# Two transfers per block instead of four for the rows of negated maxima, with the planner's costs of SP's jobs and its seeds replaced

## The reference, cut to what matters

```python
x = x + L0_attn(layernorm(x))   # one head, width 64, causal softmax
x = x + L0_ffn(layernorm(x))    # 256 x 256, inputs rounded to 8-bit floats
x = x + L1_attn(layernorm(x))   # 16 heads of width 16, rotary positions, causal softmax
x = x + L1_ffn(layernorm(x))    # sigmoid(xr Wr) * (relu(xk Wk)^2 Wv), x mixed with the row before it

scores = Q @ K^T / sqrt(d)      # per head, 2048 x 2048
scores = where(causal, scores, -inf)
out = softmax(scores) @ V
```

## Time and profile before

| | |
|---|---|
| time, median of 3 runs | 2366.51 us (2357.9 to 2366.91) |
| the profiled execution's own time | 2356.72 us |
| its span, first to last instruction | 2354.9 us |
| mean granted clock of TensorE | 0.994 of full speed |
| TensorE busy | 94% of the span |
| VectorE busy | 85% |
| ScalarE busy | 64% |
| GpSimd busy | 23% |
| DMA, mean | 53 GB/s |

### The profile page before, as it was taken

The page is one execution under the profiler, slowest core; times in us unless marked ns, Lnnn a source line. Parts: engine busy times, 40 slices in busy tenths (PEclk is TensorE's granted clock), DMA queues, the critical chain, the costliest instruction groups (busy, mean ns, idle before and its releaser), DMA issues.

```text
span 2354.9 us, 50513 instructions
## 1 busy us (share of the span) xinstructions
PE 2217.2 (94%) x19221; PEld 1031.1 (44%) x19221; DVE 2009.2 (85%) x4326; ACT 1511.1 (64%) x2753; POOL 531.2 (23%) x528
## 2 busy tenths in 40 slices
PE   7899899999999999999999999999999999999998
PEld 4555433433544444443454445444354444433354
DVE  6689899999889898888988889988887989998932
ACT  2244477676666667667656676667666677778763
POOL 5544301302322121220324212130222300000012
PEclk9999999999999999999999999999999999999999
DMA  2422411110212112021121213121021122111110
GB/s 51 115 76 60 120 49 30 42 55 13 78 45 76 42 56 73 19 78 42 31 84 42 70 37 90 33 57 57 19 55 57 38 64 68 31 36 31 30 48 30
DMA packets 185883, 125.29 MB, mean 53 GB/s; under 512 B 84912, under 2 KB 185392, under 8 KB 185648
## 3 DMA queue, kind: packets, MB, share of 16 engines
q1 hardware_dynamic: 184880, 121.16, 18.4%
q10 hardware_dynamic: 768, 0.92, 0.1%
HBM read 62.20 MB, written 59.24 MB: 52 GB/s over the span
## 4 chain that ended last, share of the span: by engine, by line
PE 61%; DVE 26%; ACT 5%; issue 3%; POOL 2%; SPq 1%; DMA 1%; POOLq 0%; DVEq 0%; ACTq 0%
DVE mx L1609 16%; PE psum L1929 15%; PE psum L1907 8%; PE psum L1875 7%; ACT probs L1372 3%; PE psum L1842 3%; PE psum L1715 2%; PE psum L1968 2%; PE psum L1777 2%; PE psum L1980 2%; PE psum L1960 2%; PE psum L1806 2%; PE psum L1746 2%; PE psum L1949 2%; PE psum L1863 2%
## 5 line engine op out<-in xcount | busy, mean ns | idle before, releaser
L1609 DVE TENSOR_REDUCE mx<-psum 128x1 f32<-128x512 f32 (+2 forms) x2304 | 1290.2, 621 | 130.4 <-PE psum L1875 89.2
L1372 ACT ACTIVATE probs<-psum 128x512 f32<-128x512 f32 x2176 | 1134.4, 607 | 325.8 <-PE psum L1907 233.3
L1929 PE MATMUL psum<-probs,vs 128*17 128x512 f32 (+3 forms) x5120 | 574.3, 535 | 1.6 <-ACT probs L1372 0.8
L1875 PE MATMUL psum<-kst,qst 48*128 48x512 f16 (+3 forms) x2560 | 425.2, 350 | 46.6 <-ACT probs L1372 16.7
L1907 PE MATMUL psum<-qst,kst 50*128 50x512 f16 (+3 forms) x2560 | 423.4, 349 | 40.9 <-DVE mx L1609 19.1
L1875 PEld LDWEIGHTS psum<-kst,qst 48*128 48x128 f16 x2560 | 127.3, 93 | 352.3 <-ACT probs L1372 127.6
L1907 PEld LDWEIGHTS psum<-qst,kst 50*128 50x128 f16 x2560 | 128.4, 93 | 331.0 <-ACT probs L1372 138.5
L1929 PEld LDWEIGHTS psum<-probs,vs 128*17 128x17 f32 x5120 | 96.3, 96 | 162.6 <-issue 123.2
L1882 PE MATMUL psum<-maskq,identh 64*128 64x64 bf16 (+1 forms) x2048 | 126.0, 202 | 0.0
L1156 POOL TENSOR_SCALAR vare<-mv 128x4 f32<-128x4 f32 x64 | 14.6, 229 | 450.9 <-DVE mv L1474 450.9
L1914 PE MATMUL psum<-maskk,identh 64*128 64x128 bf16 (+1 forms) x2048 | 112.9, 202 | 0.0
(11 more groups left out here) (173 smaller groups left out, 2820.1 us busy)
## 6 DMA issues: line engine op xcount, KB each, us to landing
qk_dram<-parts SPq DMA_DIRECT2D x168, 128.0 KB
qst<-qk_dram SPq DMA_DIRECT2D x128, 96.0 KB, 2.3
kst<-qk_dram SPq DMA_DIRECT2D x128, 96.0 KB, 2.3
v_dram<-vst SPq DMA_DIRECT2D x64, 136.0 KB, 4.0
vs<-v_dram SPq DMA_DIRECT2D x64, 136.0 KB, 2.1
xs<-x_in SPq DMA_DIRECT2D x16, 512.0 KB, 4.0
x_dram<-xs SPq DMA_DIRECT2D x16, 512.0 KB, 3.0
att_dram<-ast SPq DMA_DIRECT2D x64, 128.0 KB, 2.0
```

The lines of the kernel that those rows point to most:

```text
L1372: act.activation(dst, src, ACT.Exp, scale=DK1 ** -0.5 / LIFT ** 2).then_inc(S["exp"], 1)
L1609: ins = dve.tensor_reduce(mx1[:, n % 2, 2 * g + odd, tile % TPC, c:c + 1], bank(src, at, at + cols), AX.X, ALU.max)
L1875: ins = pe.matmul(two[odd][:, at:at + cols], qst[rows, qslot, pair, P * (tile % TPC):P * (tile % TPC + 1)], kst[rows, kslot, pair, 0:cols] ...
L1929: ins = pe.matmul(bank(7, off, CH, rows=VW, row=32 * h), vtile[:, h, :], probs[:, HG * (step_no(b, hg, k) % PSTEPS) + h, at:at + CH - off] ...
```

## The change

The rows of a block's negated maxima are laid out with the parity of head outermost and the number row next, so that 16 neighbouring partitions of `nmaxT1` go to two neighbouring partitions of `qst`. Each parity is one transfer, two per block where there were four. The waiting count per use of a slot becomes 32.

The planner gets other costs for all jobs of SP (the time for which SP is held) and for two latencies, and another list of seeds, as long as the one before. So the order of all jobs on all five engines, the bank assignments and the places of the filler matmuls are derived anew.

```diff
-SEEDS = (306, 378, 194, 6, 194, 308, 415, 291, 473, 121, 8, 110, 281, 463, 416, 413, 185, 504, 77, 23, 86, 190,
...
+SEEDS = (68, 333, 414, 370, 236, 48, 123, 291, 381, 267, 127, 221, 307, 222, 395, 39, 314, 77, 39, 284, 296,
...
-    add("SP", "load x", c, key() - (60.0 if b else 1e4), 0.1, ...
+    add("SP", "load x", c, key() - (60.0 if b else 1e4), 0.45, ...
-    add("SP", "rows0", c, key(), 0.2, ("turnmax0 d", c), ("rows0", p), last, lat=2.9)
+    add("SP", "rows0", c, key(), 1.35, ("turnmax0 d", c), ("rows0", p), last, lat=2.9)
-    add("SP", "store x2", c, key(), 0.1, ("addf", (*c, 0)), ("addf", (*c, 1)), lat=3.0)
+    add("SP", "store x2", c, key(), 0.45, ("addf", (*c, 0)), ("addf", (*c, 1)), lat=3.0)
-        add("SP", "put", (*c, bl), key(0.9), 0.5, ("res", (*c, bl)), lat=4.0)
+        add("SP", "put", (*c, bl), key(0.9), 1.87, ("res", (*c, bl)), lat=3.0)
-    add("SP", "put v", c, key(), 0.4, ("v1", (*c, 0)), ("v1", (*c, 1)), lat=4.0)
+    add("SP", "put v", c, key(), 2.1, ("v1", (*c, 0)), ("v1", (*c, 1)), lat=4.0)
-        add("SP", "load k", load, pos - LEAD - 25, 0.15, ...
+        add("SP", "load k", load, pos - LEAD - 25, 0.85, ...
-    add("SP", "load q", me, pos - LEAD - 25, 0.15, ...
+    add("SP", "load q", me, pos - LEAD - 25, 0.85, ...
-        add("SP", "load v", load, pos - 25, 0.1, ...
+        add("SP", "load v", load, pos - 25, 0.45, ...
-    add("SP", "rows", me, end - 20, 0.3, ("turnmax d", me), lat=2.6)
+    add("SP", "rows", me, end - 20, 1.35, ("turnmax d", me), lat=2.1)
-    add("SP", "put att", me, end + 2, 0.1, ("out", me), lat=3.0)
+    add("SP", "put att", me, end + 2, 0.45, ("out", me), lat=3.0)
...
-        nmaxb = sb("nmaxb", [P, MAXROWS, 2, HG // 2, TPC], F16)
+        nmaxb = sb("nmaxb", [P, 2, MAXROWS, HG // 2 * TPC], F16)
-            wt.wait_ge(f"rows {n % QRING}", 64 * (n // QRING + 1))
+            wt.wait_ge(f"rows {n % QRING}", 32 * (n // QRING + 1))
                     for odd in range(2):
-                        for row in range(MAXROWS):
-                            at = 8 * (2 * row + odd)
-                            sp.dma_start(qst[HALF * odd + PROWS + row:HALF * odd + PROWS + row + 1, n % QRING, :, :],
-                                         nmaxT1[at:at + 8, n % 2, :]).then_inc(S[f"rows {n % QRING}"], 16)
+                        first = HALF * odd + PROWS
+                        sp.dma_start(qst[first:first + MAXROWS, n % QRING, :, :],
+                                     nmaxT1[16 * odd:16 * (odd + 1), n % 2, :]).then_inc(S[f"rows {n % QRING}"], 16)
-                    link(dve.tensor_scalar(nmaxb[:, 0, :, :, :], nmax1[:, :, :, :], 1.0 / UNIT1, None, ALU.mult))
-                    ins = dve.scalar_tensor_tensor(out=nmaxb[:, 1, :, :, :].rearrange("p o g t -> p (o g t)"),
-                                                   in0=nmax1[:, :, :, :].rearrange("p o g t -> p (o g t)"), scalar=1.0 / UNIT1,
-                                                   in1=nmaxb[:, 0, :, :, :].rearrange("p o g t -> p (o g t)"),
+                    of = nmax1[:, :, :, :].rearrange("p o g t -> p o (g t)")
+                    link(dve.tensor_scalar(nmaxb[:, :, 0, :], of, 1.0 / UNIT1, None, ALU.mult))
+                    ins = dve.scalar_tensor_tensor(out=nmaxb[:, :, 1, :], in0=of, scalar=1.0 / UNIT1, in1=nmaxb[:, :, 0, :],
-                                 nmaxb[:, :, :, :, :].rearrange("p r o g t -> p (r o g t)").bitcast(BF16), identb[:, :]
+                                 nmaxb[:, :, :, :].rearrange("p o r n -> p (o r n)").bitcast(BF16), identb[:, :]
```

More of the change, by code:

```diff
@@ L458, in both @@
         return (("turned", (ln, *c)),)
-    add("SP", "load x", c, key() - (60.0 if b else 1e4), 0.1, ("store x2", p2), ("norm", p2 and (2, *p2)), lat=9.0 if c == (0, 1) else 4.0)
+    add("SP", "load x", c, key() - (60.0 if b else 1e4), 0.45, ("store x2", p2), ("norm", p2 and (2, *p2)), lat=9.0 if c == (0, 1) else 4.0)
     norm(0, ("load x", c))
@@ L558, in head_jobs @@
         old = KEYS.old[load]
-        add("SP", "load k", load, pos - LEAD - 25, 0.15, ("put", (b, load[3], 2 * (hg // 2) + 1)),
+        add("SP", "load k", load, pos - LEAD - 25, 0.85, ("put", (b, load[3], 2 * (hg // 2) + 1)),
             *[job for reader in (KEYS.readers(old) if old else []) for job in scored_with(*reader)], lat=4.5)
     slot = block_before(b, hg, q, QRING)
-    add("SP", "load q", me, pos - LEAD - 25, 0.15, ("put", (b, q, 2 * (hg // 2))),
+    add("SP", "load q", me, pos - LEAD - 25, 0.85, ("put", (b, q, 2 * (hg // 2))),
         *(scored_for(*slot) if slot else []), lat=4.5)
@@ L565, in head_jobs @@
         old = VALUES.old[load]
-        add("SP", "load v", load, pos - 25, 0.1, ("put v", (b, load[3])),
+        add("SP", "load v", load, pos - 25, 0.45, ("put v", (b, load[3])),
             *[job for reader in (VALUES.readers(old) if old else []) for job in summed_with(*reader)], lat=4.0)
@@ L631, in tail_jobs @@
     lent = (0, NQ - 1) if c == (0, 0) else None
-    add("SP", "load x2", c, key(), 0.1, ("store x2", c), ("store y", p2),
+    add("SP", "load x2", c, key(), 0.45, ("store x2", c), ("store y", p2),
         *[("put", (0, NQ - 1, bl)) for bl in (2, 3) if c in ((0, 0), (0, 1))], lat=4.0)
-    add("SP", "load att", c, key(), 0.1, *[("put att", (b, hg, q)) for hg in range(NHG)],
+    add("SP", "load att", c, key(), 0.45, *[("put att", (b, hg, q)) for hg in range(NHG)],
         ("turn", p and ("A", *p)), lat=4.0)
@@ L672, in tail_jobs @@
         add("POOL", "addv", (*c, n), key(), 1.24, ("gated", (*c, n)))
-    add("SP", "store y", c, key(), 0.1, ("addv", (*c, 0)), ("addv", (*c, 1)), lat=3.0)
+    add("SP", "store y", c, key(), 0.45, ("addv", (*c, 0)), ("addv", (*c, 1)), lat=3.0)
 def schedule():
```

## The result

The changed kernel takes 2343.66 us (median of 4 runs, 2342.86 to 2344.74), the kernel before 2362.94 us in the same set (4 runs, 2357.9 to 2366.91): ratio 0.992, 95% interval 0.9895 to 0.9945. The change saves some 19 us. The median forecast was 2352, the range 2335 to 2376.

A forecast was written before the change was run, and what follows sets the result against it. The kernel was taken as bound by the order in which TensorE and VectorE hand over PSUM banks. Gains of 1.9 + 4.4 + 7.9 = 14.2 us, ratio 0.994 on 2366.5, gave 2352 us, range 2335 to 2376.

The forecast's parts named there:

- (a): At 98.7 us `put`s issue ahead of a load of `x`; VectorE, then TensorE idle; cost 4.4 us with slower clock.
- (b): At 267 us six `put` issues stand ahead of a query load; TensorE idles 5.52 us; cost 7.9 us with slower clock.
- Sends it after one `put`, 6 to 7 us earlier: With real holding times the planner sends the late load sooner, at (a) and about as much at (b), covering either idle time.
- near 1.00: Sign of being right: TensorE's granted clock near 1.00 between 60 and 300 us.
- The term of the transfers: Two row transfers for four free SP time; worth 1.9 us, bounds 0 to 3.6 us.
- the three places on the chain: At 954, 1895 and 2150 us row transfers lie on the chain or ahead of a query load; 1.2 us less SP each.
- the second rival: Halved transfers use two DMA engines for eight, rows land up to 0.4 us later per block: 24 us lost, 2376; chance 0.08.
- the re-laying: Every job and filler matmul may move under the new order; either sign, taken as 6 us around zero.
- The backlog: Rival: new order meets a stall like (b) elsewhere, 6.3 us gain remains, 2360 us; chance 0.14.
- The bank hand-over: Rival: short waits on lines 1875 and 1907 grow, middle stretches 0.85 us worse each, 13 us slower, 2380; chance 0.16.

The follow-up runs named there:

- e3: Kernel before with three SP jobs (loads of x, query and key) moved among the `put`s, four row transfers kept: 2354.39 us, ratio 0.9955.
- e1: Kernel before with its old costs, seeds and order, only the rows of maxima in two transfers: 2358.28 us, ratio 0.9972.
- e5: Kernel before with the same three SP jobs moved as e3, plus two row transfers per block: 2348.36 us, ratio 0.9937.
- e2: Changed kernel's costs, seeds and order, but four row transfers per block as before: 2343.56 us, ratio 0.991.
- The two pairs: Two transfers, old against new SP costs at the same scatter numbers: 2537.54 against 2512.35 us (all zero), 2581.55 against 2565.12 us (random).

## Why the prediction was right

**The sign, the size class and the main cause held.** Stalls (a) and (b) were named from the earlier trace rows as the bulk of the gain, 12.3 of 14.2 us. Undone by hand they gave 6 (by the trace and at like clock) to 10.2 us (the medians of e3), with a new wait in place of a part of (b), and in the changed kernel both are gone: no wait of TensorE for a query load, none of VectorE for `x` after the first 60 us. That the forecast change, 14.2 us, lies so near the measured 19.3 (16.5 at like clock) is in part luck: the terms came out otherwise, as the next paragraphs say, and 3.6 us of the way from 2352 to 2343.66 are the base, 2366.5 where the set's median is 2362.94.

**The loads went another way than written.** "Sends it after one `put`, 6 to 7 us earlier" came true at neither place. At (a) the load leaves after two, 3.8 us earlier relative to the first. At (b) one `put` cannot be enough: the code makes that query load wait for the chunk's first `put` to land, and it leaves after three in the changed kernel, 3.5 us earlier relative to the first. e3 shows the 5.5 us wait at 1.2 with that alone. In the changed kernel TensorE has products to do meanwhile, 15.4 us of the 16 from 252 to 268 us, and waits for no query load.

**The clock came back, but not in every execution.** The text wanted "near 1.00" from 60 to 300 us. In the first profile the four stretches read 0.96 to 0.99, with 0.97 instead of 0.94 at (b) and 0.96 instead of 0.97 at (a); in the repeat of the same kernel they read 1.00, 0.96, 0.99 and 1.00, so a difference of 0.03 in one stretch of one profile says little. Idle time elsewhere still costs clock: after the 3.80 us wait for the norm eight transposes of line 1713 take 1.97 us, against 1.06 at 99.72 us.

**The term of the transfers doesn't add to the other.** It stood at 1.9 us, 3.6 at most, from the three places on the chain and TensorE's own waits. With the old order the transfers are worth 6.3 us (e1) and 6.0 (e5 under e3) by medians, 2.0 and 2.7 at like clock; with the new one nothing (e2). So in the change itself this term is nothing. The likely reason is that the two parts mend the same thing, SP held too long; that is argued, as no trace shows where e1 gains. No cost of the landing was seen: e2 and the changed kernel agree within 0.7 us, far from the 24 us of the second rival. The issue of 16 runs into two partitions holds SP for 0.617 us, not the 0.655 taken; line 1009, from which that came, itself reads 0.617 in the changed kernel.

**The failed step is the re-laying, "taken as 6 us around zero".** It was reckoned as the difference of two draws. But the new order is under other costs, and the costs of every SP job, not the `put`s alone, went from a fraction to the true time. The two pairs speak against a mere draw: 25.2 and 16.4 us at fixed scatter numbers, the second in part with a higher clock. In the changed kernel it leaves 21.7 - 10.2 = 11.5 us beyond the stalls undone by hand (10.4 at like clock), of which two transfers could have had some 3 to 6 as well. The remaining 5 to 8 us are left to the new order, where the text had zero; which hand-overs they lie in was not settled. Nor was it settled why the clock of the kernel before differs so much from one execution to the next (0.986 to 0.996) and that of the changed kernel so little, which is what their scatter goes along with.

**The rivals.** The backlog did not move: in the changed kernel TensorE has no wait for a load or a row left in its list, and the query load at (b) lands in 3.5 us. (What crowded SP there was not the first chunks of all four batches, as the text has it, but chunks (0,0) and (0,3) of the first batch, whose `put`s e3 names.) The bank hand-over did not grow: 61.0 us for 62.5, a middle stretch of 57.39 us for 57.20, and the worst at 55.5 for 55.3.

## What to carry to other kernels

Where an order is fixed ahead of time, a job that is costed too low does harm far from itself: compare planned and real holding times of every queue, the idle-looking ones too, before tuning the order. Two edits that relieve the same resource are not to be added up; try each alone and both. Where one kernel's runs scatter, put the granted clock beside each time before taking a difference of medians for an effect. When the large waits for transfers are gone, look for an engine that runs longer than its own median beside another engine's work.

## What the hardware showed that was not expected

One kernel's time followed the mean granted clock of the execution: 2357.0 us at 0.996, 2373.7 at 0.987, the same order in both. A norm of one tile takes 0.38 to 0.41 us alone and up to 1.9 beside GpSimd, and it waits out GpSimd's instructions, fills (0.95 us) as well as sums (1.26 us). And a transfer twice as large from SBUF to SBUF holds SP no longer: 0.617 us for 4 KB into two partitions, 0.627 for 2 KB into one.
